# When GpSimd may send each group of row scatters in the dispatch of a mixture-of-experts layer

## The reference

```
x = x + attention(layernorm(x), adj)        # 8 heads, masked by the graph's adjacency
x = x + ffn(layernorm(x))
# ffn, per token:
shared = gelu(t @ W1s + b1s) @ W2s + b2s     # hidden width 512, for every token
rw = softmax(t @ Wr); topw, topi = top_k(rw, 2); topw /= sum(topw)
routed = sum over the 2 chosen of 8 experts: topw * (gelu(t @ W1p[e] + b1p[e]) @ W2p[e] + b2p[e])
ffn(t) = shared + routed
```

## Time and profile before

| | us |
|---|---|
| median of 3 runs | 1715.22 |
| lowest and highest run | 1707.22, 1719.48 |
| the profiled execution's own time | 1720.02 |
| its span, first to last instruction | 1718.2 |

### The profile page before, as it was taken

The page is one execution under the profiler, slowest core; times in us unless marked ns, Lnnn a source line. Parts: engine busy times, 40 slices in busy tenths (PEclk is TensorE's granted clock), DMA queues, the critical chain, the costliest instruction groups (busy, mean ns, idle before and its releaser), DMA issues. The chain is left out here.

```text
span 1718.2 us, 34370 instructions
## 1 busy us (share of the span) xinstructions
PE 1244.3 (72%) x9895; PEld 731.1 (43%) x9896; DVE 1080.2 (63%) x2270; ACT 1010.6 (59%) x1745; POOL 946.4 (55%) x969
## 2 busy tenths in 40 slices
PE   4899999999999992099997000298998989999500
PEld 2566666666666662044443000154444444444200
DVE  2777887878877874756665000166676757666478
ACT  2677777777777774288775000177776767777300
POOL 2354555545554545466566777455676666666700
PEclk9999999999999995599998555599999999999755
DMA  1143223222233202232221111122222222222099
GB/s 46 30 102 87 68 68 80 68 68 68 75 99 84 68 19 81 67 87 83 79 85 60 53 53 53 55 74 69 73 81 62 74 72 78 71 74 72 16 283 303
DMA packets 193906, 136.82 MB, mean 80 GB/s; under 512 B 14863, under 2 KB 176318, under 8 KB 193868
## 3 DMA queue, kind: packets, MB, share of 16 engines
q1 hardware_dynamic: 159820, 94.10, 21.5%
q0 software_dynamic: 17408, 33.87, 5.9%
q10 hardware_dynamic: 16640, 8.39, 1.6%
HBM read 66.52 MB, written 71.86 MB: 81 GB/s over the span
## 5 line engine op out<-in xcount | busy, mean ns | idle before, releaser
L837 DVE SCALAR_TENSOR_TENSOR h<-hid,h 128x512 f16<-128x512 f32 x416 | 283.6, 691 | 197.1 <-ACT h L817 153.0
L1031 POOL DMA_INDIRECT pairs_dram<-x_rows x288 | 307.5, 1068 | 91.6 <-issue 90.9
L778 PE MATMUL Z<-xTu,w 128*128 128x512 f16 x1248 | 307.1, 391 | 33.3 <-ACT hid L828 16.0
L895 POOL DMA_INDIRECT slots_dram<-x_rows,pair_slot x256 | 249.2, 973 | 117.0 <-issue 72.1
L789 PE MATMUL Y<-h,w 128*128 128x512 f16 x1248 | 297.1, 388 | 19.9 <-issue 16.8
L817 ACT ACTIVATE h<-hid 128x512 f16<-128x512 f32 x416 | 262.0, 630 | 81.5 <-PE Z L778 28.1
L828 ACT ACTIVATE hid<-Z,biases 128x512 f32<-128x512 f32 x416 | 280.1, 673 | 0.2 <-issue 0.2
L364 DVE TENSOR_REDUCE smax<-S 128x8 f32<-128x1024 f32 x128 | 156.8, 1225 | 112.4 <-PE S L530 112.2
L789 PEld LDWEIGHTS Y<-h,w 128*128 (+1 forms) x1248 | 123.0, 100 | 186.7 <-issue 57.7
L778 PEld LDWEIGHTS Z<-xTu,w 128*128 (+1 forms) x1248 | 117.5, 99 | 176.3 <-issue 48.4
L827 ACT ACTIVATE turn<-biases 128x1 f32<-128x1 f32 x104 | 20.8, 200 | 272.6 <-PE Z L778 210.7
(11 more groups left out here) (140 smaller groups left out, 2098.4 us busy)
## 6 DMA issues: line engine op xcount, KB each, us to landing
x_rows<-slots_dram SPq DMA_DIRECT2D x72, 260.0 KB
slots_dram<-blank SPq DMA_DIRECT2D x13, 1300.0 KB, 9.7
y_pairs<-pairs_dram SPq DMA_DIRECT2D x32, 512.0 KB, 7.5
x_res<-in_x_dram SPq DMA_DIRECT2D x32, 256.0 KB, 2.9
adj<-in_adj_dram SPq DMA_DIRECT2D x32, 256.0 KB, 3.2
xT_dram<-xT SPq DMA_DIRECT2D x32, 256.0 KB, 3.2
xTu<-xT_dram SPq DMA_DIRECT2D x32, 256.0 KB
out_dram<-x_res ACTq DMA_DIRECT2D x16, 512.0 KB, 7.4
```

The source lines that it names most:

```text
L778: mm = pe.matmul(self.Z[:, c], self.w1[:, k, :, c * P:(c + 1) * P][:, e, :], self.xT[:, b, m], start=n == 0, stop=n == 2)
L837: dve.scalar_tensor_tensor(out=self.h16[:, b, 1, c], in0=self.hid[:, c], scalar=HS, in1=self.h16[:, b, 0, c], op0=ALU.mult, op1=ALU.subtra ...
L895: pool.indirect_dma_start(slots_dram, bass.IndirectOffsetOnAxis(ap=pair_slot[:, t, k:k + 1], axis=0), row_words[:, t, :], None).then_inc(r ...
L1031: pool.indirect_dma_start(pairs_dram, bass.IndirectOffsetOnAxis(ap=pair_of[n][:, j:j + 1], axis=0), y_sb[n][:, j], None, bounds_check=TOP ...
```

## The change

The wait on z_ps is asked for both choices, once for every second group. Group u of choice k is the (32k+u)-th of 64 groups, and it waits, where u is even, for the first chunk of shared unit (32k+u)/2. So each shared unit releases eight scatters in place of four, and the last of the 64 groups are released by shared unit 31. The waits on row_sent, the order of the scatters and the copy between the choices stay as they are.

```diff
         for k in range(TOP):
             for u in range(NG):
-                if k == 0:
-
-                    pool.wait_ge(f.z_ps, u * FC + 1)
+                if u % TOP == 0:
+
+                    pool.wait_ge(f.z_ps, (k * NG + u) // TOP * FC + 1)
                 for j in range(GT):
                     t = u * GT + j
                     if k or u:
```

## The result

| | before | with the change |
|---|---|---|
| median of 20 runs, us | 1713.14 | 1722.61 |
| lowest and highest | 1702.61, 1726.65 | 1713.69, 1729.10 |
| profiled execution, its span | 1720.02, 1718.2 | 1720.20, 1718.4 |

The ratio is 1.0063, with a 95% interval of 1.0045 to 1.0082. The change makes the kernel slower by a little over half a per cent, where 33 us less were forecast, and the time lies outside the range.

A forecast was written before the change was run, and what follows sets the result against it. GpSimd's list of 256 scatters, 731.78 to 1095.77 us, was taken as the bound. Removable waits of 40.8 us, less 6.1 issue and 1.1 contention, left 33.6; 33.5 off 1715.2 gave 1681.7 us, range 1671 to 1695.

The forecast's parts named there:

- The list counted afresh: GpSimd's scatter list: 322.6 us of steps, 6.3 contention and 2.0 middle stop make 330.9 against 364.0, last scatter at 1062.7.
- steps 4 and 5: Scatter list: contention beside the shared expert, 1.1 us for 28 more scatters; the middle stop for landings and copy stays.
- Step 4: Scatters beside the shared expert cost 0.039 us more each; 28 more of them there cost 1.1 us.
- The landings rival: In the dispatch, later landings make row_sent hold scatters at the old pace of up to 1.575 us; 1715 us, chance 0.03.
- Step 6: The shared expert does not wait for the scatters; even if they slow it, it has 120 us of cover.
- Step 3: New gates in the dispatch cost nothing: units take about 6.1 us, eight scatters 10.1 us, so GpSimd falls behind the gates.
- steps 1 and 2: First-half waits on z_ps hold 44.0 us; 20 of 21 go, 40.8 us, less 6.1 of returning issue time, leaving 34.7.
- The slower rival: VectorE's low-part copies (L837) hold up GpSimd's scatters beside the shared expert, at most 0.691 us each; kernel slower, chance 0.02.

The follow-up runs named there:

- e18: The changed kernel measured once more, on a chip of the fast kind: 1621.6 us against 1630.8 for the kernel before, ratio 0.9946.
- e7: The changed kernel without any wait on z_ps in the dispatch, slow kind: 1852.6 us against 1704.3 for the kernel before, ratio 1.0841.
- e9: The changed kernel without waits on z_ps, with a 128x512 GpSimd addition behind every four scatters, slow kind: 1743.9 us against 1704.3 for the kernel before.
- e8: The changed kernel with GpSimd additions replacing the scatters beside the shared expert, true scatters afterwards, slow kind: 2007.3 us against 1704.3 for the kernel before.
- e1: The changed kernel without any wait on z_ps in the dispatch, fast kind: 1618.5 us against 1630.9 for the kernel before, ratio 0.9924.
- e11: The changed kernel with SyncE sending the tiles beside the shared expert, GpSimd scattering afterwards, slow kind: 1849.7 us against 1713.8 for the kernel before.
- e3: The changed kernel without waits on z_ps, with a 128x512 GpSimd addition behind every four scatters, fast kind: 1684.3 us against 1630.9 for the kernel before.

## Why the prediction was wrong

**What bounds the kernel** (GpSimd's list from 732 to 1096, the shared expert over long before) was read rightly for the kernel before.

**The list counted afresh** (255 steps of 1.265 us, with steps 4 and 5) holds where nothing else interferes: in e18 the last scatter starts at 1063.9 against 1062.7 forecast, with contention and the middle stop in it (e18's wait for the landings there was 1.8 us). Step 4's contention was somewhat larger than its 0.039 us for each scatter: the first 128 of e18 take 1.324 us a step where the free ones took 1.265 in the kernel before, and L895's mean beside the shared expert is 1.01 us, not 0.985. The landings rival stayed away: e18 has 24 waits on landings of 0.3 us each, in place of the ordinary issue time and not on top of it.

**Step 6 is the one that failed**: "the shared expert does not wait for the scatters", with 120 us of cover and "nothing points there". It does wait, not through a semaphore or a buffer of its own but through the delivery of TensorE's counts. On three of five chips that delivery stalls when GpSimd issues indirect DMAs back to back, and does not with a pause of about 1.2 us behind every four (e7 against e9). The change allowed sixteen in a row in place of four or eight. The shared expert fell to 11.8 us for each unit, all the cover was used up, and it ended after the scatters.

**Step 3 failed with it.** It took the gate times of the kernel before, 6.1 us a unit, as given, and had GpSimd fall behind them. But the units stretched until the gates bound again. In the changed kernel GpSimd issues sixteen scatters (20.2 us), then stands at the gate some 3 us, the counts arrive, and two units are released: 23 us, the same 1.44 us a scatter as the kernel before needed in all (364.0 / 255 = 1.43). So nothing was gained. The closest of the sentences on record was that the effect would be of the landings rival's kind "if the new gate bound after all", with a reason that was not the true one.

**The 44.0 us of steps 1 and 2 were misread too**, as time that a faster gate gives back. On the fast kind the change gains 9.2 us, and its list reaches the length of the forecast, so the list before must have been shorter there; no profile of it exists. TensorE's units run at 5.6 us on that kind (the adds of e18 from 750 to 912), and the old gates would open sooner. An estimate for the list before is 31 x 5.6 up to the last gate, 3.8 for the three scatters behind it, 3.3 for the middle stop and 160.7 for the second choice, 341 us in all, against 332.4. On the slow kind the units of the kernel before took 6.1 us, and part of that was its own doing: behind the four scatters from 812.25 GpSimd stopped at 817.0, the matmul of the count that it waited for had ended at 817.2, and the count came at 818.1.

**What the trace of before showed of it.** The "issue" rows and the mean of L895 were the place where contention was looked for, on GpSimd's side. The victim was TensorE. In the kernel before, ScalarE had three waits in the shared stretch (840 to 935) that no instruction's end explains:

```profile
ACT h L817 <- remote: 8.9, 3, 3.0
```

Asking why a wait for TensorE ends when no row of TensorE ends would have led to the late counts, and to a rival in which denser scatters slow the shared expert.

**The slower rival** had GpSimd held up by VectorE. L895's mean is 975 ns in the changed kernel and 973 before, so nothing of it came. The loss ran the other way, from GpSimd's issuing to TensorE. The runs e8 and e9 show that the port rule of the Trainium skill, cited with e8, does act between GpSimd's additions and VectorE; for the scatters it decides nothing here.

**What is not shown.** By what path GpSimd's issuing holds TensorE's counts back, and why two chips of five are free of it, stays open. Since the ends of matmuls are modelled, it is open too whether the count alone is late or the last writes of its matmul. Whether the stops or the mean pace of the scatters decide was not separated, as said with e9. Open is also whether the routed block's extra 53 to 82 us on the slow kind (499 to 526 against 444 to 446) come from late counts. They do occur there: in 400 us of the routed block 151 of TensorE's 341 counts on the trace are over 0.1 us late in the kernel before, the longest by 7.2 us, and none of 461 on the fast kind (e1, e18). GpSimd's stop behind each four scatters has a median of 0.95 us in that block. ScalarE's waits there are in part ended by "remote", and on the fast kind (e1) none is. A pause long enough to tell, 1.2 us behind every two scatters, was not tried there.

## What to carry to other kernels

When work is packed more densely on one engine, look for what other engines would lose by it, also where no semaphore joins them, and treat a wait that ends where no instruction ends as a measurement of that. A gate that looks like lost time may be the pause that keeps another engine running: before it is taken out, put a pause of the same length in its place and see what the pause alone is worth. Here a pause of 1.24 us behind every four scatters kept the shared expert at 5.97 us for each unit where none made it 77. And a saving of this kind should be measured on more than one chip: this change gains 0.5% on one kind and loses 0.6% on the other.

## What the runs showed of the hardware

- On three of five chips that ran these kernels, TensorE's semaphore counts arrive late while GpSimd issues indirect DMAs 0.30 us apart (0.96 us each). Without a pause TensorE's work goes at 77 us for a unit where 5.6 are needed. ScalarE's and VectorE's own counts, so far as the trace has them, came on time (197 of 197 in the changed kernel).
- With a stop of 1.24 us in GpSimd's issuing behind every four such DMAs of the dispatch it is gone (e9: 1 of 125 counts over 0.1 us late). A stop of 0.39 us does not do it, and with 1.24 us behind eight it builds up over some 50 us and then tips. The mean pace of the DMAs changed along with the stops.
- Also in the routed block of the slow kind TensorE's counts are late, 151 of 341 in the kernel before; on the fast kind none of 461 is.
- 8 bytes or 520 bytes a row make no difference (shared expert over at 1102 and 1109). The same tiles sent by SyncE, with 137 GB/s moved in all, or arithmetic on GpSimd, do nothing to TensorE's counts (none of 187 late in e11 and in e8).
- Additions of 128x512 on GpSimd raise the mean of VectorE's L837 from 693 ns to about 880 ns with one behind every four scatters (735 to 920 of e3 and e9, on both kinds of chip) and to 1468 ns with nothing but additions (735 to 950 of e8).
- The kernel before itself takes 1631 us on the fast kind and 1704 to 1730 on the slow one.
